# Moving sixteen weight picks to the end of the experts, reordering the stages of the last tiles, and adding 24 unit-matrix products

## What is computed

```
x = x + tanh(g_xattn) * attention(layernorm(x), ctx, ctx)   # 8 heads, softmax(q k / sqrt(8)) v
h = layernorm(x)
probs = softmax(h @ router_weight.T)                        # 64 experts
top_v, top_i = top_k(probs, 8)                              # not renormalised
for e in range(64):
    gate, up = split(h @ gate_up[e].T)                      # 2 x 128
    y_e = (silu(gate) * up) @ down[e].T
x = x + tanh(g_ffn) * sum over a token's 8 experts of top_v * y_e
```

## Time and profile before

| | |
|---|---|
| median of three runs | 745.96 us |
| the profiled execution's own time | 742.97 us |
| its span, first to last instruction | 741.1 us |
| mean granted clock of PE | 0.894 of 2.4 GHz |
| attention and routing, to the last product of the table | about 366 us |
| the change over, to the first expert's first product | to 383 us |
| the experts | to about 688 us |

### The profile page before, as it was taken

The page is one execution under the profiler, slowest core; times in us unless marked ns, Lnnn a source line. Parts: engine busy times, 40 slices in busy tenths (PEclk is TensorE's granted clock), DMA queues, the critical chain, the costliest instruction groups (busy, mean ns, idle before and its releaser), DMA issues.

```text
span 741.1 us, 14594 instructions
## 1 busy us (share of the span) xinstructions
PE 558.6 (75%) x4132; PEld 444.8 (60%) x4132; DVE 486.2 (66%) x1324; ACT 444.7 (60%) x935; POOL 366.7 (49%) x441
## 2 busy tenths in 40 slices
PE   0399898988989898674248787887877888776476
PEld 0265565655656565442048776787877877776365
DVE  2568788788787878532567666666667676664356
ACT  4467677677676767451217666666667676665910
POOL 8412166566565645455704555555555555555200
PEclk9999999899898989775559999999999999998599
DMA  6888888778675769611356777767777777755796
GB/s 139 194 211 212 193 239 227 191 209 211 192 206 174 183 151 319 249 65 72 112 149 192 225 211 209 236 189 213 220 222 215 222 212 206 215 153 165 271 422 258
DMA packets 71793, 151.08 MB, mean 204 GB/s; under 512 B 13273, under 2 KB 37871, under 8 KB 70208
## 3 DMA queue, kind: packets, MB, share of 16 engines
q1 hardware_dynamic: 52912, 101.90, 49.7%
q0 software_dynamic: 16208, 45.42, 18.0%
q10 hardware_dynamic: 2624, 3.15, 1.9%
HBM read 90.34 MB, written 64.26 MB: 209 GB/s over the span
## 4 chain that ended last, share of the span: by engine, by line
PE 30%; DVE 22%; ACT 17%; another core or an unknown queue 11%; issue 10%; DMA 6%; POOL 1%; SPq 1%; ACTq 1%; DVEq 0%; POOLq 0%
DVE MX L838 9%; PE ST L1476 6%; PE OX L1493 5%; PE SC L1685 5%; ACT PE_T L1377 4%; PE SC L1456 4%; DMA ACC_B<-y_rows 4%; PE ST L1697 3%; ACT PE_T L1262 3%; ACT XTP L1343 2%; ACT WP L1350 2%; PE OX L1697 2%; DVE XTP L1073 2%; PE ST L1671 2%
## 5 line engine op out<-in xcount | busy, mean ns | idle before, releaser
L779 POOL DMA_INDIRECT y_rows<-PE_T,IDXE x128 | 135.0, 1055 | 143.8 <-ACT XTP L1343 68.2
L1262 ACT ACTIVATE PE_T<-ST 128x512 f32<-128x512 f32 x256 | 139.3, 598 | 81.8 <-PE ST L1476 70.4
L838 DVE TENSOR_REDUCE MX<-SC 128x4 f32<-128x1024 f32 x128 | 154.4, 1215 | 50.4 <-PE SC L1456 44.8
L725 POOL DMA_INDIRECT x_rows<-XN,IDX x128 | 125.9, 984 | 95.2 <-PE ST L1476 37.7
L1685 PE MATMUL SC<-XTP,WP 128*128 128x320 f32 x768 | 132.4, 323 | 0.6 <-issue 0.5
L1476 PE MATMUL ST<-QC,KP 128*128 128x256 f32 x512 | 114.3, 341 | 12.9 <-ACT PE_T L1262 9.7
L1685 PEld LDWEIGHTS SC<-XTP,WP 128*128 128x128 f32 x768 | 122.7, 202 | 1.4 <-issue 1.0
L1476 PEld LDWEIGHTS ST<-QC,KP 128*128 128x128 f32 x512 | 80.4, 209 | 52.8 <-ACT PE_T L1262 26.2
L1456 PE MATMUL SC<-KP,QC 32*128 32x256 f32 x512 | 62.6, 345 | 51.5 <-DVE MX L838 25.6
L1094 DVE TENSOR_TENSOR PE_T<-SC,PE_T 128x320 f32<-128x320 f32 x64 | 31.4, 491 | 94.1 <-ACT PE_T L1357 71.7
L1671 PE MATMUL ST<-IDENT,XE 128*128 128x128 f32 x256 | 45.2, 287 | 50.8 <-DVE XTP L1073 39.1
(11 more groups left out here) (164 smaller groups left out, 806.4 us busy)
## 6 DMA issues: line engine op xcount, KB each, us to landing
W<-experts_dram SPq DMA_DIRECT2D x64, 384.0 KB
XE<-x_rows SPq DMA_DIRECT2D x64, 288.0 KB
x_rows<-FILL POOLq DMA_DIRECT2D x16, 576.0 KB
ACC_B<-y_rows SPq DMA_DIRECT2D x9, 1024.0 KB, 15.2
QC<-q_scr SPq DMA_DIRECT2D x56, 128.0 KB
X<-x_rows SPq DMA_DIRECT2D x64, 72.0 KB
k_scr<-KS SPq DMA_DIRECT2D x16, 256.0 KB
q_scr<-QS SPq DMA_DIRECT2D x16, 256.0 KB
```

What stands on the lines that cost most here:

```text
L725: pool.indirect_dma_start(x_rows, bass.IndirectOffsetOnAxis(ap=IDX[:, rows, k:k + 1], axis=0), XN2[:, rows, :], None).then_inc(dispatched[ ...
L779: pool.indirect_dma_start(y_rows, bass.IndirectOffsetOnAxis(ap=IDXE[:, n % YS, j:j + 1], axis=0), Y[:, n % YS, j, :], None, bounds_check=T ...
L838: nc.vector.tensor_reduce(MX[:, u // 4].rearrange("p r (j g) -> p j r g", j=2)[:, :, :, group(u) % 4], SC[:, u % 2, :, :].rearrange("p j ( ...
L1262: nc.scalar.activation(PE_T[:, h % EXP_RING, :], ST[:, j, :], ACT.Exp, scale=SCALE).then_inc(exp_done, 1)
```

## The change

Three things are changed, and nothing of the arithmetic that reaches the output.

1. `FIRST_PICKS` falls from 32 to 16. The 16 picks for which there is then no place ahead of the experts go to the last eight experts, two in each step; the loop's picks keep their number.
2. The hand-written order of the last tiles' stages changes on PE, ACT, DVE and POOL.
3. Ahead of the first `rows_t`, PE multiplies the unit matrix by itself 24 times into `OX`, which nothing reads before it is written again.

```
-            end(TILES - 4, 2, TILES - 3)
-            end(TILES - 3, 0, TILES - 2)
-            end(TILES - 2, 2, TILES - 1)
+            end(TILES - 4, 1, TILES - 3)
+            end(TILES - 3, 1, TILES - 2)
+            end(TILES - 2, 3, TILES - 1)
             end(TILES - 1)
...
-            FIRST_PICKS = 2 * (TILES * K8 // 2 - (E - 2 * SLOTS))
+            FIRST_PICKS = 2 * SLOTS
...
-                if not isinstance(i, int):
+                if not isinstance(i, int) or i > 0:
                     order_weight(i * 2 + (FIRST_PICKS - 2 * SLOTS) // K8 + n // 4, i * (2 * SLOTS) + FIRST_PICKS - 2 * SLOTS + n * 2 + a)
...
             exps(T, 0)
             turned_sums(Turn(t + 2 + 2))
+            exps(T, 1)
             normalise2(Turn(t + 1 + 3))
-            exps(T, 1)
             put_max(T, -1, 1)
+            exps(T, 2)
             copy_xt(Turn(t + 1 + 3))
-            exps(T, 2)
             exps(T, 3)
...
+            for _ in range(24):
+                nc.tensor.matmul(OX[:, 0:P], IDENT[:, :], IDENT[:, :], start=True, stop=True)
             for n in range(2):
                 rows_t(0, n)
```

More of the change, by code:

```diff
@@ L1017, in _ @@
             chosen(t + 1)
+            placed(t + 1)
             attended(t + 2)
-            placed(t + 1)
             chosen(t + 2)
+            placed(t + 2)
             weigh(Turn(t + 3 + 2))
-            placed(t + 2)
             attended(t + 3)
@@ L1621, in _ @@
             turn_sums(Turn(t + 2 + 2))
+            second_scores(T, 2)
             end_rows(t + 1)
-            second_scores(T, 2)
+            second_scores(T, 3)
             end_logits_of(t + 1)
-            second_scores(T, 3)
             end_outputs(t + 2)
             second_scores(T, 4)
+            end_before(t + 1)
             sums(T, -1, 0)
-            end_before(t + 1)
             second_scores(T, 5)
@@ L1637, in _ @@
             sums(Turn(t + 3 + 2), -2, 3)
+            end_before(t + 2)
             turn_sums(Turn(t + 3 + 2))
-            end_before(t + 2)
             end_outputs(t + 3)
```

## The result

The changed kernel takes 738.68 us (median of 12 runs, 731.91 to 741.14), the kernel before 743.16 us in the runs beside it (12 runs, 739.70 to 746.63). The ratio is 0.9925, with a 95% interval of 0.9899 to 0.995: faster by 4.5 us between the medians and 5.6 us (3.7 to 7.5) by the ratio. That is less than 1%, on the side that was forecast, and 738.7 stands beside a forecast of 738.9. Measured against the larger sample of the kernel before, the forecast gain was 7.1 and the measured one 4.5 to 5.6.

The account below looks back on a forecast made before the run. Up to the change over, POOL's queue and its two waits bound, then the chain ACT, DVE, PE. 3.9 + 0.75 + 3.1 - 0.2 - 0.1 = 7.4, taken as 7.1: 738.9 us, range 733.5 to 745.5.

Parts of the forecast that it names:

- Part 1, the order: POOL's queue over the last tiles: the new order starts tile 15 3.9 us sooner; bounds 2.5 and 7.9.
- The idle ahead of tile 13: POOL's 2.39 us wait for tile 13's destination rows from DVE: cancelled by the new order, no idle left.
- the late report at tile 15's sums: Last sums before ACT's copy: PE reports them about 4 us late, and nothing in the change touches this.
- Part 2, the picks: DVE ahead of the first low part: 16 fewer picks gain 0.75 us; the 16 in the last eight cost 0.1.
- Part 3, the products: 24 unit products ahead of the first rows raise PE's clock: 3.1 us gained, bounds 0 to 3.3; 0.2 us delay.
- the clock falls back before it is used: Rival, between unit products and expert 0's first product: Part 3 brings nothing, gain 4.4, time 741.5 us; chance 0.18.
- the late sums gone: Rival, attention's last sums reported in time: tile 15 starts 7.9 us sooner, gain 11.0 at most, 735 us; chance 0.22.
- Expert 0's gate and up: Sign on PE: first twelve products in 1.8 us, not 3.2; wrong if the clock of 383 to 387 stayed at 0.50.
- the pieces at L1357: Sign at ACT's silu: 21 waits for an unnamed releaser, 64.3 us; the prediction would be wrong if their number changed.
- The idle ahead of tile 14: Sign in POOL's timeline: the 5.43 us wait for tile 14's destination rows falls under 2 us.

Follow-up runs that it names:

- order_only: The kernel before with the new order of the last tiles alone, 32 picks ahead, no unit products: 733.85 us, ratio 0.994 to the kernel before.
- hold_clock: The changed kernel with 8 more unit products between the first and second expert's turns: 729.44 us, ratio 0.9907 to the kernel before.
- step_product: The changed kernel with one more unit product ahead of each of 64 experts' down product: 726.57 us, ratio 0.9845 to the kernel before.
- picks_only: The kernel before with the moved picks alone, 16 ahead and 16 in the last eight experts: 734.12 us, ratio 0.9979 to the kernel before.
- order_picks: The changed kernel without its unit products: 729.47 us, ratio 0.9902 to the kernel before; a second time, on the third group's chip, 628.76 us, 0.996.
- picks_none: The changed kernel with no pick ahead of the experts, those 16 in the first eight experts: 727.81 us, ratio 0.9874 to the kernel before.
- hold_none: The changed kernel with 8 more products between the first two turns and no pick ahead, third group's chip: 627.93 us, ratio 0.9942 to the kernel before.
- after_again: The changed kernel itself, unchanged, run again on the third group's chip: 628.83 us, ratio 0.9943 to the kernel before.

## Why the prediction was right

**Part 1, the order: right in size, and in mechanism but for the place of the late report.** Forecast 3.9 us by POOL's timeline and queue. The single profile of the changed kernel gave 2.2, but over all profiles of the chips with late reports the stretch from tile 12 to tile 15 is 42.6, 42.3 and 42.4 us with the old order and 38.5 on average with the new (40.4, 38.7, 37.9, 38.2, 37.9, 38.0, 38.8): 3.9. The idle ahead of tile 13 went to 0.16 or 0.17 in all of them. Tile 14 was forecast 26.9 us behind tile 12 and came 25.7 to 28.2 behind it. But I had said that nothing in the change touches the late report at tile 15's sums. In four of the seven new profiles (the changed kernel, order_only, hold_clock, step_product) no wait for an unnamed releaser stands at their copy (L1243); it stands at tile 15's exponentials (L1262), some 12 us sooner, and is 5.8 to 6.9 us long. The size came out although the report moved, and that part is luck. Without any late report, on the third chip, the stretch is 35.2 to 35.9.

**Part 2, the picks: right alone, incomplete together.** 0.67 us measured for 0.75. What the working left out is that the parts interact: with the new order alone, 32 picks cost 2.6 us (order_only). I had checked that 16 picks end in time, so the sum was right, but order and picks can't be taken one without the other. In the last eight, where I took 0.1, no cost is shown.

**Part 3, the products: the step that failed.** Their length was right, 8.07 us for 8.1, with the clock rising 5.2 us after their start (363.7 to 368.9), and they were hardly in the way. The saving was forecast at 3.1 of 3.3 us. It was 0.9 from the first rows to expert 1 (8.13 to 7.22), and the first rows themselves came 0.5 us later (16.9 to 17.4). The rival "the clock falls back before it is used" came true, with 0.18 of the chances. It was priced with nothing left of the gain; in fact the turns of experts 0 and 1 still had the full clock and gate and up lost it, so part stayed. I chose against it because PE had been all idle in the fall at 343.3 in the kernel before. In the changed kernel PE stood idle for only 1.97 us, with turns before and behind, and the clock fell all the same.

**The sum.** Up to tile 15 it is 3.9 us by the means. From there to expert 1's first product it is 26.75 us before and 24.62 in the changed kernel, 2.1 less: 0.7 by the picks as picks_only has them, 0.4 by the products, and 1.0 that came only with order and picks together. Of that 1.0, 0.4 lie in the first rows and 0.6 in a clock that rose sooner (3.2 us behind the first gate product in order_picks, over 4.2 in picks_only); two profiles don't tell it from scatter. Together that is 6.0 us where 7.55 were forecast (3.9 + 0.75 + 3.1 - 0.2); the medians say 4.5 and the ratio 5.6 (3.7 to 7.5). 7.1 is inside that interval, near its edge. That 738.7 stands so near 738.9 is partly luck: the first three runs before had a median 2.8 us above the one of twelve, and that made up for the saving that Part 3 missed.

**A wrong sum in a rival.** For the late sums gone, 7.9 + 0.75 + 3.1 is 11.75 and not 11.0, which gives 734.2 and not 735.

**The signs of being wrong.** Two of those that the prediction named came. Expert 0's gate and up ran mostly at the low clock (0.61 from 376 to 380), which is Part 3's failure. And the pieces at L1357 changed, 26 and not 21 (79.8 us and not 64.3), yet the 62 experts took only 0.85 us longer; the other old-order profiles have 19 and 16 and the other new-order ones 12 to 22, so their number is scatter and no effect of the change. Their sum is not a price either: a wait that another engine's work would have filled costs nothing. The idle ahead of tile 14 was listed as under 2 us; the prediction's own working has 4.0 (341.0 to 345.0), and it was 5.34 here and 2.8 to 3.8 in the other six.

## What to carry to other kernels

When work is held back by two chains that meet, moving one of them forward shifts the price of everything that hangs on the other: price the parts of a change together, at the place where they join. A TensorE that was brought to full clock ahead of time can lose it again before the work comes: with only turns and a wait of 2 to 4 us between it did so in five of six kernels here, and with eight small products in that wait in none of three. But hold the gain against the noise: 1.6 us of such a clock was not to be seen in a time of 630. And before several per cent of a trace are explained by the program, run it on a second chip: here 80 us of the experts' time stayed on the first ones.

## What the hardware showed that I had not expected

- The same program took 738.7 us on one chip and 628.8 on another, the kernel before 743.2 and 632.5. On the slower chips reports of PE's products reach ACT (and, a few times in a profile, DVE) about 3.2 us late, about once in 9.5 us for long parts of the experts, up to 6.9 us in attention. In the four profiles of the fast chip there is none. What delays them is open, and so is how much of the difference they cause.
- PE's own records don't show the delay where it happens. In the kernel before, the gate and up of one expert has its last record before 418.5, its silu starts at 421.59 after 3.25 us of idle with an unnamed releaser, and PE has records from 418.30 to 421.94 without a gap; its own wait (1.85 us) comes only behind that. The idle time of ACT with an unnamed releaser is what gives it away.
- With the new order, the first rows start 16.7 to 16.9 us behind tile 15's first dispatch without unit products (three profiles) and 17.0 to 18.0 with 24 of them (seven). In four of the seven PE had ended the products and still waited for the load (1.20 us in picks_none, 0.92 in hold_none, 0.67 in after_again, 0.44 in step_product), so standing in the way isn't the whole cause. With the old order the products changed nothing there (17.4 against 17.4 and 17.5). It wasn't tried further.
